# Projections that load x by columns, with means and deviations made a chunk ahead and spread through DRAM

## The chip, the cores and the metric

The program runs on one core of one Trainium2 chip. The metric is the device time of one execution in microseconds; three runs of the kernel before gave 1718.45 to 1718.74, with a median of 1718.49.

## The reference

A gated cross-attention block with a feed-forward part behind it, on 4 sequences of 1024 tokens with 512 features. This case is about its first lines, the projections:

```python
def _layernorm(x, axis=-1, eps=1e-05):
    m = jnp.mean(x, axis=axis, keepdims=True)
    v = jnp.var(x, axis=axis, keepdims=True)
    return (x - m) / jnp.sqrt(v + eps)
...
Q = heads(layernorm(x), Wq, bq)     # [4096 tokens, 512]
K = heads(ctx, Wk, bk)
V = heads(ctx, Wv, bv)
scores = Q @ K^T / sqrt(32) + adj;  scores = where(mask == 0, -inf, scores)
out = softmax(scores) @ V
x = x + tanh(g_xattn) * (out @ Wo.T + bo)
x = x + tanh(g_ffn) * ffn(layernorm(x))   # three cycles of a small network
```

## The kernel before

`project_phase` is the first of the program's stages; `attention_phase` and the feed-forward stage follow. The projections go through the 4096 tokens in 8 chunks of 512. For each chunk TensorE makes twelve products of 128 x 512 outputs (`acc`, four PSUM banks in turn): four of K from the context, four of V, four of Q from the normalised x. A product sums over four tiles t of 128 features, and every float32 operand is split into a high and a low part (`_hi`, `_lo`), so that each product is 4 x 3 = 12 matmuls (`three_pass`, L164 to L166): 144 matmuls a chunk. The context comes already with its features on the partitions (`ctxT`); x comes by rows (tokens on the partitions).

So x is normalised by rows and then turned on TensorE:

- VectorE's `norm_stats` reads the x rows of a chunk (`x_raw`) with BN_STATS and BN_AGGR, which give a mean and a variance for each token in `mv` (L448, L452).
- GpSimd's `inverse_std` makes 1/sqrt(variance + eps) in `rstd` (L256, L258).
- VectorE's `norm_apply` makes `xn` (L460), and TensorE turns it with 16 transposes of 128 x 128 into the PSUM tile `x_t` (L363), between the K and the V products.
- ScalarE makes `xT_hi` from it (L425), VectorE `xT_lo` (L497), and the Q products read both.

ScalarE also rounds each product into `out_hi` (L416) and the next context into `c_hi` (L402); VectorE makes `out_lo` (L488), `c_lo` (L465) and the V output (L503). Each of these reads frees a PSUM bank by `acc_read`; product n waits for the read of product n - 4. SyncE's queue stores the outputs.

GpSimd's queue loads x rows, context, mask and adjacency, and between the loads GpSimd builds one tile of `am` (the mask turned into a large negative number and added to adj) with two operations (`mask_tile`, L267 and L270). Its program runs in order: for chunk c it waits for `xn` of the chunk before, loads `x_raw` and `c_raw`, makes the deviations, loads mask and adjacency and builds. At c = 4 it also loads what the first attention group needs (`first_group`, L276 to L279).

Nothing plans this order at run time: each engine has its own written program, and semaphores join them. Chunks 1 to 7 are loops on SyncE and TensorE, chunks 1 to 6 on ScalarE and VectorE. The line that holds the turn in place on VectorE is, in `chunk`,

```python
if more:
    norm_stats(c + 1)
    split_context(c + 1)
    norm_apply(c + 1)
low_parts(c, 8, 4, bias_q)
```

## Time and profile before

| | |
|---|---|
| median of 3 runs | 1718.49 us |
| the profiled execution | 1718.82 us, its span 1717.0 us |
| TensorE (PE) busy | 1693.4 us, 99% |
| VectorE (DVE) busy | 1454.5 us, 85% |
| ScalarE (ACT) busy | 1270.9 us, 74% |
| GpSimd (POOL) busy | 663.3 us, 39% |
| projections, from the first record to the first matmul of the attention | 0 to 289.28 us |

PE's matmuls overlap in the records, so that the time which one takes in a row of them is the distance between two starts, not its own duration. PEld is TensorE's loading of weights. A timeline row says when an instruction (or a merged run of x of them) started and how long it ran, and in brackets how long its engine had been idle and who released it.

### The profile page before, as it was taken

The numbers are of one execution on the slowest core, as the hardware profiler recorded it, in microseconds if no ns is written. First come the engines' busy times: TensorE is split into PE (matmuls) and PEld (weight loads), VectorE is DVE, ScalarE is ACT, GpSimd is POOL, SyncE is SP. The second block draws the span as 40 slices with busy tenths as digits, with TensorE's granted clock in tenths as the row PEclk, the third lists the DMA queues.
The fourth block names the chain that finished last, engine by engine and source line by source line (L and its number), as shares of the span: only waits on it lengthen the run. The fifth ranks groups of instructions, "written<-read, shape, count | busy, mean of one in ns | idle before, by whom it ended". The sixth has DMA issues, their size and how long they took to land. (4 is left out here: it accounts for less than half of the span.)

```text
span 1717.0 us, 34356 instructions
## 1 busy us (share of the span) xinstructions
PE 1693.4 (99%) x12456; PEld 1295.8 (75%) x12456; DVE 1454.5 (85%) x2580; ACT 1270.9 (74%) x2249; POOL 663.3 (39%) x598
## 2 busy tenths in 40 slices
PE   9999999999999999999999999999999999999997
PEld 7888888777777777777777777777786685775873
DVE  6554554999999999999999999999778978969968
ACT  4222223999999999999999999999765576466557
POOL 3442341432368642487532796454323010100100
PEclk9999999999999999999999999999999999999998
DMA  7778675866366675378563676665424313411301
GB/s 281 273 243 295 226 265 169 191 166 155 103 180 180 133 169 130 113 211 179 130 162 97 183 189 131 150 136 152 150 67 160 90 50 98 139 50 50 114 25 50
DMA packets 162105, 258.92 MB, mean 151 GB/s; under 512 B 25616, under 2 KB 78096, under 8 KB 161952
## 3 DMA queue, kind: packets, MB, share of 16 engines
q1 hardware_dynamic: 110416, 158.84, 29.1%
q0 software_dynamic: 50960, 97.01, 24.7%
q8 instruction: 93, 1.52, 0.4%
q10 hardware_dynamic: 576, 1.05, 0.2%
q14 instruction: 60, 0.49, 0.1%
HBM read 168.47 MB, written 84.18 MB: 147 GB/s over the span
## 5 line engine op out<-in xcount | busy, mean ns | idle before, releaser
L1024 DVE CUSTOM_DVE_ANT_0 a_neg<-a_sc_ps,am 128x1024 f32<-128x1024 f32 x512 | 621.7, 1214 | 1.4 <-PE a_sc_ps L856 1.3
L964 ACT ACTIVATE a_prob<-a_neg,a_row_min 128x1024 f32<-128x1024 f32 x512 | 585.7, 1144 | 13.9 <-DVE a_row_min L1024 7.8
L870 PEld LDWEIGHTS a_tr_ps<-ident,a_prob 128*128 128x128 f32 x4096 | 461.0, 140 | 89.1 <-issue 53.2
L870 PE MATMUL a_tr_ps<-ident,a_prob 128*128 128x128 f32 x4096 | 519.8, 274 | 0.9 <-ACT a_probT L942 0.9
L999 DVE COPY a_probT<-a_tr_ps 128x512 f32<-128x512 f32 x512 | 350.7, 685 | 36.9 <-PE a_tr_ps L870 35.4
L942 ACT ACTIVATE a_probT<-a_tr_ps 128x512 f32<-128x512 f32 x512 | 304.0, 594 | 35.1 <-PE a_tr_ps L870 16.0
L752 POOL DMA_DIRECT2D a_q_st<-q_parts x144 | 79.8, 560 | 161.2 <-PE a_sc_ps L856 125.3
L856 PE MATMUL a_sc_ps<-k_first,a_q_st 96*128 96x512 f32 x384 | 126.2, 426 | 0.0
L856 PE MATMUL a_sc_ps<-a_k_st,a_q_st 96*128 96x512 f32 x384 | 126.0, 426 | 0.0
L890 PE MATMUL a_o_ps<-a_probT,a_v 128*32 128x256 f32 x2048 | 123.6, 382 | 0.6 <-ACT a_o L953 0.6
L890 PE MATMUL a_o_ps<-a_probT,v_first 128*32 128x256 f32 x2048 | 123.8, 382 | 0.0
L890 PEld LDWEIGHTS a_o_ps<-a_probT,a_v 128*32 128x32 f32 x2048 | 60.5, 109 | 55.9 <-ACT a_probT L942 12.0
L890 PEld LDWEIGHTS a_o_ps<-a_probT,v_first 128*32 128x32 f32 x2048 | 60.0, 109 | 56.1 <-DVE a_probT L999 11.6
L757 POOL TENSOR_SCALAR a_m_raw<-a_m_raw 128x1024 f32<-128x1024 int32 x24 | 87.0, 3632 | 27.0 <-DMA a_m_raw<-mask 26.8
L964 ACT ACTIVATION_READ_ACCUMULATOR a_prob<-a_neg,a_row_min 128x1 f32 x512 | 97.1, 190 | 0.0
L132 POOL TENSOR_TENSOR st_o<-st_o,st_rinv 128x512 f32<-128x512 f32 x32 | 41.5, 1298 | 114.4 <-DMA st_rinv<-rinv_all 114.3
L1711 DVE TENSOR_TENSOR f_B<-f_B,f_acc 128x512 f32<-128x512 f32 x64 | 43.7, 683 | 33.5 <-PE f_acc L166 24.3
L488 DVE SCALAR_TENSOR_TENSOR p_out_lo<-p_acc,p_bias_k,p_out_hi 128x512 fp32r<-128x512 f32 x32 | 23.7, 750 | 55.2 <-ACT p_out_hi L416 55.2
L416 ACT ACTIVATE p_out_hi<-p_acc,p_bias_q 128x512 fp32r<-128x512 f32 x32 | 21.9, 689 | 62.9 <-PE p_acc L166 62.9
L402 ACT ACTIVATE p_c_hi<-p_c_raw 128x2048 fp32r<-128x2048 f32 x7 | 13.4, 1918 | 72.7 <-PE p_acc L166 58.6
L1493 ACT ACTIVATE f_xn<-x,f_shift,f_rstd 128x512 f32<-128x512 f32 x32 | 23.5, 805 | 57.8 <-POOL f_shift L1296 57.8
L416 ACT ACTIVATE p_out_hi<-p_acc,p_bias_k 128x512 fp32r<-128x512 f32 x32 | 21.7, 689 | 58.6 <-PE p_acc L166 52.7
(236 smaller groups left out, 3364.2 us busy)
## 6 DMA issues: line engine op xcount, KB each, us to landing
a_q_st<-q_parts POOLq DMA_DIRECT2D x144, 128.0 KB, 4.0
k_first<-k_parts POOLq DMA_DIRECT2D x24, 512.0 KB, 7.9
a_k_st<-k_parts POOLq DMA_DIRECT2D x24, 512.0 KB, 7.9
a_m_raw<-mask SPq DMA_DIRECT2D x24, 512.0 KB, 5.0
a_adj_raw<-adj SPq DMA_DIRECT2D x24, 512.0 KB, 5.9
k_parts<-p_out_hi SPq DMA_DIRECT2D x32, 256.0 KB, 6.0
k_parts<-p_out_lo SPq DMA_DIRECT2D x32, 256.0 KB, 6.3
v_all<-p_v_out SPq DMA_DIRECT2D x8, 1024.0 KB, 4.4
```

The source lines that it names most:

```text
L132: pool.tensor_tensor(w.o[:], w.o[:], w.rinv[:], ALU.mult).then_inc(w.step, 1)
L416: act.activation(out_hi[:, m, :], acc[:, (n0 + m) % 4, :], ACT.Identity, bias=bias[:, m:m + 1]).then_inc(hi_ready, 1)
L752: pool.dma_start(q_st[qb][quad * D:(quad + 1) * D], src).then_inc(q_loaded[qb], 16)
L757: pool.tensor_scalar(m_raw[:, t % 2, :].bitcast(F32), m_raw[:, t % 2, :], 0.0, -BIG, ALU.is_equal, ALU.mult).then_inc(big_ready, 1)
L856: last = pe.matmul(sc_ps[:, r % 2, half * 512:(half + 1) * 512], q_st[qb][0:STACK, h, qt * P:(qt + 1) * P], k_st[par][0:STACK, h, half * 5 ...
L870: last = pe.transpose(tr_ps[:, bank(u, half), j * P:(j + 1) * P], prob[:, r % NPROB, t * P:(t + 1) * P], ident[:])
L890: last = pe.matmul(o_ps[h * D:(h + 1) * D, 0:QB], v_sb[vpar][:, t, h * D:(h + 1) * D], probT[:, prev % 2, h, t, :], start=(t == 0), stop=( ...
L942: act.activation(probT[:, (r // UB) % 2, h, 0:4, qt * P:(qt + 1) * P], tr_ps[:, bank(u, 0), :].rearrange("p (t q) -> p t q", t=4), ACT.Cop ...
L964: act.activation(prob[:, r % NPROB, :], neg[:, r % 2, :], ACT.Exp, scale=-1.0, bias=row_min[:, r % 2:r % 2 + 1], accum_out=row_sum[:, r // ...
L999: dve.tensor_copy(probT[:, (r // UB) % 2, h, 4:8, qt * P:(qt + 1) * P], tr_ps[:, bank(u, 1), :].rearrange("p (t q) -> p t q", t=4)).then_i ...
L1024: dve.tensor_tensor_reduce(out=neg[:, r % 2, :], in0=sc_ps[:, r % 2, :], in1=am[:, 2 * qb + qt, :], scale=-1.0, scalar=3.4e38, op0=ALU.add ...
L1711: dve.tensor_tensor(target[j][:, m, :], target[j][:, m, :], acc[:, 2 + step // 2, :], op).then_inc(shared_read, 1)
```

## The change

Chunk 0 goes as before. From chunk 1 on x is loaded by columns: a second input, `xT`, holds x with the features on the partitions, 512 tokens a chunk, and `x_cols` (the same memory as `xn`) takes it. The x rows are still loaded, for the means and variances alone. TensorE's 16 transposes of chunks 1 to 7 go. In their place:

- GpSimd's `inverse_std` writes mean and inverse deviation of a chunk's tokens into columns 0 to 3 and 4 to 7 of `norm_cols` (128 x 32), with a third small operation for the mean.
- VectorE's `turn_norm` turns `norm_cols` in squares of 32 x 32 into `norm_turned`.
- GpSimd stores it in DRAM with four DMAs of 8 x 32 elements (`store_norm`), waits until they have landed, and loads the two rows of 512 back into all 128 partitions (`spread_norm`, to `norm_rows`, in the second half of the memory of `stage[:, 0]`).
- VectorE subtracts the mean row (`centre`) and multiplies by the deviation row (`scale`), one operation of 128 x 512 each for each of the four feature tiles.
- ScalarE and VectorE split `x_cols` instead of `x_t`.

`norm_stats(c + 1)` stands at the start of chunk c, `turn_norm(c + 1)` after the second K output. GpSimd's program issues its loads first and builds the mask tile behind them; the three parts of `first_group` are apart, behind the masks of chunks 3, 4 and 5. The loops over chunks are written out. The two gates' loads count on `b_loaded`.

```diff
-                held_wait(pool, mv_ready, c + 1, pool_passed)
+                wait(pool, mv_ready, c + 1)
                 pool.tensor_scalar(var_eps[:], mv[:, :, 1], EPS, 1.0, ALU.add, ALU.mult).then_inc(var_ready, 1)
-                pool.wait_ge(var_ready, c + 1)
-                pool.tensor_tensor(rstd[:], var_eps[:], minus_half[:], ALU.pow).then_inc(rstd_ready, 1)
+                pool.tensor_scalar(mean, mv[:, :, 0], 1.0, 0.0, ALU.mult, ALU.add).then_inc(var_ready, 1)
+                pool.wait_ge(var_ready, 2 * c + 2)
+                pool.tensor_tensor(rstd, var_eps[:], minus_half[:], ALU.pow).then_inc(rstd_ready, 1)
...
+            def load_rows(c):
+                pool.wait_ge(stats_ready, c)
                 pool.dma_start(x_raw[:], x[ds(c * CH, CH), :].rearrange("(t p) e -> p t e", p=P)).then_inc(x_loaded, 16)
...
+            def load_columns(c):
+                pool.wait_ge(xT_lo_ready, ET * c)
+                pool.dma_start(x_cols[:], xT[c].rearrange("(t p) s -> p t s", p=P)).then_inc(xT_loaded, 16)
+
+            def store_norm(c):
+
                 inverse_std(c)
-                mask_tile(c)
+                pool.wait_ge(turned, c)
+                target = stat_rows[c].rearrange("k (t g j) -> g (k t) j", g=P // SQUARE, j=SQUARE)
+                for g in range(P // SQUARE):
+                    pool.dma_start(target[g], norm_turned[g * SQUARE:g * SQUARE + 2 * TT, :]).then_inc(norm_stored, 16)
+
+            def spread_norm(c):
+                wait(pool, scaled, ET * (c - 1))
+                pool.wait_ge(norm_stored, 64 * c)
+                pool.dma_start(norm_rows, stat_rows[c].partition_broadcast(P)).then_inc(norm_rows_loaded, 16)
+
+            inverse_std(0)
+            pool.wait_ge(xn_ready, 1)
+            load_rows(1)
+            load_context(1)
+            pool.wait_ge(w_lo_ready, 2 * ET)
+            load_mask(0)
+            load_columns(1)
+            store_norm(1)
+            load_rows(2)
+            spread_norm(1)
+            build_mask(0)
+            for c in range(1, NCH):
+                if c < NCH - 1:
+                    load_context(c + 1)
+                load_mask(c)
+                if c < NCH - 1:
+                    store_norm(c + 1)
+                    if c < NCH - 2:
+                        load_rows(c + 2)
+                    spread_norm(c + 1)
+                    load_columns(c + 1)
+                build_mask(c)
+                if c == 3:
+                    first_keys()
+                elif c == 4:
+                    first_queries()
+                elif c == 5:
+                    first_values()
...
-                pe.wait_ge(xn_ready, c + 1)
-                for t in range(ET):
-                    for s in range(TT):
-                        last = pe.transpose(x_t[:, t, s * P:(s + 1) * P], xn[:, s, t * P:(t + 1) * P], ident[:])
-                    last.then_inc(xT_ready, 1)
                 if first:
+                    pe.wait_ge(xn_ready, 1)
+                    for t in range(ET):
+                        for s in range(TT):
+                            last = pe.transpose(x_t[:, t, s * P:(s + 1) * P], xn[:, s, t * P:(t + 1) * P], ident[:])
+                        last.then_inc(xT_ready, 1)
...
-            with pe.Fori(1, NCH) as c:
+            for c in range(1, NCH):
                 chunk(c, False)
...
+                        act.wait_ge(scaled, ET * (c - 1) + t + 1)
+                        source = x_cols
+                    act.activation(xT_hi[:, t, :], source[:, t, :], ACT.Copy).then_inc(xT_hi_ready, 1)
...
+            def centre(c, t):
+                if t == 0:
+                    dve.wait_ge(xT_loaded, 16 * c)
+                    dve.wait_ge(norm_rows_loaded, 16 * c)
+                dve.tensor_tensor(x_cols[:, t, :], x_cols[:, t, :], norm_rows[:, 0, :], ALU.subtract).then_inc(centred, 1)
+
+            def scale(c, t):
+                dve.wait_ge(centred, ET * (c - 1) + t + 1)
+                dve.tensor_tensor(x_cols[:, t, :], x_cols[:, t, :], norm_rows[:, 1, :], ALU.mult).then_inc(scaled, 1)
...
+            def turn_norm(c):
+                dve.wait_ge(rstd_ready, c + 1)
+                wait(dve, norm_stored, 64 * (c - 1))
+                dve.transpose(norm_turned[:], norm_cols[:]).then_inc(turned, 1)
...
+                    if normalised:
+                        centre(c, m)
+                        if m:
+                            scale(c, m - 1)
+                        if m == 1 and c < NCH - 1:
+                            turn_norm(c + 1)
 
             def chunk(c, more):
-                low_parts(c, 0, 0, bias_k)
...
+                if c and more:
+                    norm_stats(c + 1)
+                low_parts(c, 0, 0, bias_k, c > 1)
+                if c == 1:
+                    turn_norm(2)
+                    for t in range(ET):
+                        centre(1, t)
+                        if t:
+                            scale(1, t - 1)
+                if c:
+                    scale(c, ET - 1)
...
-                    dve.tensor_tensor(xT_lo[:, t, :], x_t[:, t, :], xT_hi[:, t, :].bitcast(F32), ALU.subtract).then_inc(xT_lo_ready, 1)
...
+                    dve.tensor_tensor(xT_lo[:, t, :], (x_cols if c else x_t)[:, t, :], xT_hi[:, t, :].bitcast(F32), ALU.subtract).then_inc(xT_lo_ready, 1)
...
+                if c == 0:
+                    norm_stats(1)
                 wait(dve, v_stored, 16 * c)
                 for m in range(4):
                     dve.wait_ge(acc_ready, NACC * c + 4 + m + 1)
                     dve.tensor_tensor(v_out[:, m, :], acc[:, m, :], bv_rows[:], ALU.add).then_inc(acc_read, 1)
+                    if c == 0 and m == 1:
+                        turn_norm(1)
                 if more:
-                    norm_stats(c + 1)
                     split_context(c + 1)
-                    norm_apply(c + 1)
                 low_parts(c, 8, 4, bias_q)
```

VectorE, the second half of chunk 0, before: the outputs of V, then statistics, context and normalisation of chunk 1, then the low parts of Q.

```order
L497 TENSOR_TENSOR p_xT_lo<-p_x_t,p_xT_hi 128x512 x4
L503 TENSOR_TENSOR p_v_out<-p_acc,p_bv_rows 128x512 x4
L448 BN_STATS p_stats<-p_x_raw 128x6 x4
L452 BN_AGGR p_mv<-p_stats 128x2 x4
L465 TENSOR_TENSOR p_c_lo<-p_c_raw,p_c_hi 128x2048
L460 TENSOR_SCALAR p_xn<-p_x_raw,p_mv,p_rstd 128x512 x4
L488 SCALAR_TENSOR_TENSOR p_out_lo<-p_acc,p_bias_q,p_out_hi 128x512 x4
```

The same place in the changed kernel (`p_norm_cols` holds mean and inverse deviation).

```order
L574 TENSOR_TENSOR p_xT_lo<-p_x_t,p_xT_hi 128x512 x4
L495 BN_STATS p_stats<-p_x_raw 128x6 x4
L499 BN_AGGR p_mv<-p_stats 128x2 x4
L582 TENSOR_TENSOR p_v_out<-p_acc,p_bv_rows 128x512 x2
L543 STREAM_TRANSPOSE p_norm_turned<-p_norm_cols 128x32
L582 TENSOR_TENSOR p_v_out<-p_acc,p_bv_rows 128x512 x2
L521 TENSOR_TENSOR p_c_lo<-p_c_raw,p_c_hi 128x2048
L549 SCALAR_TENSOR_TENSOR p_out_lo<-p_acc,p_bias_q,p_out_hi 128x512 x4
L495 BN_STATS p_stats<-p_x_raw 128x6 x4
L499 BN_AGGR p_mv<-p_stats 128x2 x4
```

The statistics of chunk 1 moved ahead of V's outputs, the normalisation of rows is gone, and the next statistics stand behind the Q parts. In chunk 2 of the changed kernel VectorE's program reads as follows, from its third K output on; `p_xn` is the memory of `x_cols` and `p_stage` that of `norm_rows`.

```order
L543 STREAM_TRANSPOSE p_norm_turned<-p_norm_cols 128x32
L549 SCALAR_TENSOR_TENSOR p_out_lo<-p_acc,p_bias_k,p_out_hi 128x512
L513 TENSOR_TENSOR p_xn<-p_xn,p_stage 128x512
L517 TENSOR_TENSOR p_xn<-p_xn,p_stage 128x512
L549 SCALAR_TENSOR_TENSOR p_out_lo<-p_acc,p_bias_k,p_out_hi 128x512
L513 TENSOR_TENSOR p_xn<-p_xn,p_stage 128x512
L517 TENSOR_TENSOR p_xn<-p_xn,p_stage 128x512 x2
L574 TENSOR_TENSOR p_xT_lo<-p_xn,p_xT_hi 128x512 x4
L582 TENSOR_TENSOR p_v_out<-p_acc,p_bv_rows 128x512 x4
L521 TENSOR_TENSOR p_c_lo<-p_c_raw,p_c_hi 128x2048
```

Here the low parts of K have the two steps of normalisation between them, and `xT_lo` reads two tiles in SBUF. GpSimd's program for one chunk, before:

```order
L286 DMA p_x_raw<-x 128x4x512
L288 DMA p_c_raw<-ctxT 128x4x512
L256 TENSOR_SCALAR p_var_eps<-p_mv 128x4
L258 TENSOR_TENSOR p_rstd<-p_var_eps,p_minus_half 128x4
L263 DMA p_stage<-mask 128x1024
L264 DMA p_stage<-adj 128x1024
L267 TENSOR_SCALAR p_stage<-p_stage 128x1024
L270 TENSOR_TENSOR am<-p_stage 128x1024
```

And in the changed kernel:

```order
L292 DMA p_c_raw<-ctxT 128x4x512
L264 DMA p_stage<-mask 128x1024
L265 DMA p_stage<-adj 128x1024
L256 TENSOR_SCALAR p_var_eps<-p_mv 128x4
L257 TENSOR_SCALAR p_norm_cols<-p_mv 128x4
L259 TENSOR_TENSOR p_norm_cols<-p_var_eps,p_minus_half 128x4
L304 DMA stat_rows<-p_norm_turned 8x32 x4
L288 DMA p_x_raw<-x 128x4x512
L309 DMA p_stage<-stat_rows 128x1024
L296 DMA p_xn<-xT 128x4x512
L269 TENSOR_SCALAR p_stage<-p_stage 128x1024
L271 TENSOR_TENSOR am<-p_stage 128x1024
```

The two building operations went from behind their own loads to the end of the chunk's list, behind the load of the columns, and six DMAs are new.

## Rows read from the trace of the kernel before

**Rows 1.** The page: busy time by engine, then TensorE's granted clock in 40 slices.

```profile
PE 1693.4 (99%) x12456; PEld 1295.8 (75%) x12456; DVE 1454.5 (85%) x2580; ACT 1270.9 (74%) x2249; POOL 663.3 (39%) x598
...
PEclk9999999999999999999999999999999999999998
```

**Rows 2.** Busy time in a stretch, chunks 1 to 7.

```profile
core 0: us, PE busy (x) PEld busy (x) DVE busy (x) ACT busy (x) POOL busy (x), PEclk, DMA share, GB/s
...
44.00:286.00 242.00, 241.09 (x1119) 200.79 (x1119) 120.47 (x194) 63.75 (x92) 79.69 (x57) 1.00 0.70 248
```

**Rows 3.** Timeline of TensorE: first K product of chunk 2, its turn, first V product.

```profile
79.49 0.39 PE L164 MATMUL p_acc<-p_c_hi,p_w_hi 128*128 128x512 f32 x1
...
90.37 1.91 PE L363 MATMUL p_x_t<-ident,p_xn 128*128 128x128 f32 x16
92.04 0.47 PE L164 MATMUL p_acc<-p_w_hi,p_c_hi 128*128 128x512 f32 x1
```

**Rows 4.** Timeline of ScalarE: the context's high part, in chunks 2 and 3.

```profile
68.87 1.92 ACT L402 ACTIVATE p_c_hi<-p_c_raw 128x2048 fp32r<-128x2048 f32 x1 [10.06 <-PE p_acc L166]
...
103.31 1.92 ACT L402 ACTIVATE p_c_hi<-p_c_raw 128x2048 fp32r<-128x2048 f32 x1 [10.09 <-PE p_acc L166]
```

**Rows 5.** Timeline of TensorE: chunk 0's first Q product, into chunks 1 and 4.

```profile
33.17 0.39 PE L164 MATMUL p_acc<-p_xT_hi,p_w_hi 128*128 128x512 f32 x1
...
43.83 0.39 PE L166 MATMUL p_acc<-p_xT_lo,p_w_hi 128*128 128x512 f32 x1
44.95 0.49 PE L164 MATMUL p_acc<-p_c_hi,p_w_hi 128*128 128x512 f32 x1 [0.74 <-DVE p_out_lo L488]
...
148.11 0.39 PE L166 MATMUL p_acc<-p_xT_lo,p_w_hi 128*128 128x512 f32 x1
148.66 0.49 PE L164 MATMUL p_acc<-p_c_hi,p_w_hi 128*128 128x512 f32 x1 [0.17 <-DVE p_out_lo L488]
```

**Rows 6.** Timeline of VectorE in chunk 0.

```profile
26.12 2.47 DVE L497 TENSOR_TENSOR p_xT_lo<-p_x_t,p_xT_hi 128x512 fp32r<-128x512 f32 x4
...
33.98 2.46 DVE L448 BATCH_NORM_STATS2 p_stats<-p_x_raw 128x6 f32<-128x512 f32 x4
...
36.77 4.25 DVE L465 TENSOR_TENSOR p_c_lo<-p_c_raw,p_c_hi 128x2048 fp32r<-128x2048 f32 x1
42.24 1.91 DVE L460 TENSOR_SCALAR p_xn<-p_x_raw,p_mv,p_rstd 128x512 f32<-128x512 f32 x4 [1.22 <-POOL p_rstd L258]
```

**Rows 7.** Timeline of GpSimd: a mask tile, a blocked and an unblocked deviation.

```profile
32.75 3.66 POOL L267 TENSOR_SCALAR p_stage<-p_stage 128x1024 f32<-128x1024 int32 x1 [10.00 <-DMA p_stage<-mask]
36.49 2.40 POOL L270 TENSOR_TENSOR am<-p_stage 128x1024 f32<-128x1024 f32 x1
...
72.49 2.13 POOL L256 TENSOR_SCALAR p_var_eps<-p_mv 128x4 f32<-128x4 f32 x1 [17.22 <-DVE p_mv L452]
...
142.09 0.20 POOL L256 TENSOR_SCALAR p_var_eps<-p_mv 128x4 f32<-128x4 f32 x1 [16.06 <-DVE p_mv L452]
142.37 1.04 POOL L258 TENSOR_TENSOR p_rstd<-p_var_eps,p_minus_half 128x4 f32<-128x4 f32 x1
```

**Rows 8.** Timeline of VectorE in chunk 2, and two starts in chunk 0.

```profile
6.10 0.69 DVE L476 TENSOR_TENSOR p_w_lo<-p_stage,p_w_hi 128x512 fp32r<-128x512 f32 x1
6.70 0.68 DVE L474 TENSOR_TENSOR p_c_lo<-p_c_raw,p_c_hi 128x512 fp32r<-128x512 f32 x1
...
72.31 2.26 DVE L465 TENSOR_TENSOR p_c_lo<-p_c_raw,p_c_hi 128x2048 fp32r<-128x2048 f32 x1
...
91.30 0.75 DVE L488 SCALAR_TENSOR_TENSOR p_out_lo<-p_acc,p_bias_k,p_out_hi 128x512 fp32r<-128x512 f32 x1 [1.98 <-ACT p_out_hi L416]
```

**Rows 9.** The x rows' DMA issued at 19.19 us: KB, us from issue to landing.

```profile
p_x_raw<-x POOLq DMA_DIRECT2D x1, 1024.0 KB, 6.7
```

**Rows 10.** The context tile's DMA landings over all chunks; GpSimd's time for three issues.

```profile
DMA to landing us min/median/max: 4.1/10.1/16.3
...
L278 POOL DMA_DIRECT2D q_first<-q_parts x3 | 1.6, 552 | 0.0
```

110 lines of the change are left out of this document (54 added, 56 removed).

## The prediction

> **What bounds the kernel now.** I read the page first [rows 1]: TensorE is busy for 99% of the span at its upper clock (2.4 GHz, a granted clock of 0.9 or more in all slices but the last), and the other engines have room. The change is inside the projections, so I looked at that stretch alone [rows 2]: from 44 to 286 us TensorE is busy for 241.1 of 242.0 us, VectorE for 120.5, ScalarE for 63.8, GpSimd for 79.7, and the DMA engines are 0.70 busy at 248 GB/s. So here the end is set by what TensorE has to do, and only what is taken out of its queue, or put into it as a wait, moves the time. Behind the projections nothing is edited; TensorE stays the busy engine there, and its work starts when the projections end. An us saved ahead of it is an us saved.
>
> **What TensorE loses.** In chunk 2 the first K matmul starts at 79.49 and the 16 transposes start at 90.37, 48 matmuls later: 10.88 / 48 = 0.2267 us each [rows 3]. The first V matmul starts at 92.04, so the transposes hold the queue for 1.67 us. The whole cadence is better read from one event of each chunk: the context's high part starts at 68.87 in one and at 103.31 in the next [rows 4], 34.44 us. 144 matmuls are 144 x 0.2267 = 32.64 us. The rest, 1.80 us, is what a turn costs (the two or three matmuls behind it start a little apart: 0.13 us more than the 1.67). Seven chunks lose it: 7 x 1.80 = 12.6 us. The upper bound is this; the lower is 7 x 1.67 = 11.7.
>
> **Two stalls that go.** Into chunk 1 TensorE waits: the matmul ahead starts at 43.83, the next at 44.95, where 44.06 would be the cadence [rows 5]. What it waits for is the first low part of Q, which VectorE does at about 44.07 only, because the normalisation of rows stands ahead of it from 42.24, and before that the context's low part took 4.25 us [rows 6]. `norm_apply` goes out of this place, so the low part is made as soon as ScalarE's half is there. That is 0.89 us, and 0.1 for the slower start after it. Into chunk 4 it is 148.11 to 148.66 [rows 5]: 0.32 and 0.1. That one comes from the loads of the first group, put all at once ahead of x and context; they are now spread over three chunks. Together 1.4 us.
>
> **What is added, and what hides it.** On VectorE a chunk loses `norm_apply` (about 1.9 us [rows 6]) and gets eight operations of 128 x 512 with two inputs in SBUF. The same shape stood in chunk 0: starts at 6.10 and 6.70, so 0.6 us each [rows 8], 4.9 us for eight. 120.5 us in seven chunks becomes about 120.5 + 6 x 3 + 5, 144 of 228 us: there is room, so only the places matter. I count from the first K matmul of a chunk (t = 0), with times of chunk 2 [rows 3, 8]: K's last low part runs from 91.30 - 79.49 = 11.8 to 12.6; V's products are due from 13.6 on (no turn between now), Q's first matmul at 2 x 10.88 = 21.8, the next chunk at 32.6.
>
> Chunks 2 to 7: the last low part of Q ends 1.7 into the next chunk, as K's does after its product (92.05 against 90.37). The statistics take 36.77 - 33.98 = 2.8 us [rows 6], to 4.5. K's low parts then have centre and scale between them, 0.75 + 0.6 + 0.6 = 2.0 us for each 2.72 us of TensorE. After the last, scale ends at 14.4, ScalarE's last `xT_hi` at 15.0, `xT_lo` at 15.7: 6.1 us ahead of the Q products at 21.8. V's outputs then run from 15.7, their first bank needed at 21.8. The turn of the statistics waits for GpSimd: unblocked 0.2 + 0.2 + 1.04 = 1.4 us after 4.5 [rows 7], blocked twice as at 72.49 (2.13) it would be 5.3. VectorE comes to the turn at 8.3, so it waits between nothing and 1.5 us; the slack of 6.1 takes both. Nothing on the path.
>
> The turn itself has no row. It is not cheaper than nothing and the nearest whole operation, on a 16 times wider tile, is 0.6 us; I take 0.1, near the aggregation's size, and both bounds are inside the slack. The Trainium skill, "VectorE: DVE Perf Modes", section "The three transpose paths", gives 311 ns for a VectorE transpose of 128 x 128 in bf16, and no run here shows one yet; by that figure nothing in the sum changes either.
>
> Chunk 1 is tighter: all eight operations stand behind the K parts. 12.6 + 0.1 to 0.6 + 4.9, then 0.6 on ScalarE and 0.7 on VectorE for the last tile, gives 18.9 to 19.4, and with the first V output, 0.7 more, 19.6 to 20.1 against 21.8. Slack 1.7 us or more. I cost it at nothing.
>
> Chunk 0: the statistics of chunk 1 now stand ahead of V's outputs. `xT_lo` ends at 28.6 [rows 6]; the x rows land at 19.19 + 6.7 = 25.9 [rows 9], so the statistics end at 31.4 and the first V output at 32.1. Its bank is needed by the first Q matmul at 33.17 [rows 5]: slack 1.0. After the second V output VectorE waits for GpSimd's 1.4 us and turns, at about 33.2; the third output's bank is needed two products later, at 38.6. Nothing again, but this is the smallest slack for an event that rests on a DMA.
>
> GpSimd gets, a chunk, one small operation (0.2 us unblocked, 2.1 blocked), four small DMAs, a broadcast and a column load: six issues of 0.53 us as for q_first [rows 10], 3.2 us. 79.7 us in 242 leave room for 5. In order on its queue: the stores go out by 11, it waits for them to land before the broadcast, then loads the columns once `xT_lo` is done (15.7), then builds the mask, 3.65 + 2.40 us [rows 7], to about 23.5. The waits on landing hold only the column load and the mask behind them. Both loads are needed by VectorE's first centre of the next chunk, at 32.6 + 5.3 = 37.9: 21 us after issue, against landings of 4.1 to 16.3 us for a tile of that size [rows 10]. The data a chunk moves rises from 34.44 x 0.248 = 8.5 MB by 1.0 (columns) and 0.5 (broadcast) to 10.1 MB, in 32.6 us 310 GB/s; at the same GB/s a share that is a DMA share of 0.87. High, not full.
>
> **The shared port.** The mask's second operation ran from 36.49 to 38.89, and VectorE's `c_lo` beside it took 4.25 us in place of 2.26 [rows 6 to 8]; the other way round GpSimd's tiny operation took 2.13 us beside a `c_lo` in place of 0.20. So an operation with two SBUF inputs on VectorE and one on GpSimd do not run together. The change makes twelve more such operations on VectorE a chunk (centre, scale, and `xT_lo`, which read PSUM). That is why the mask's place counts: at 17.4 to 23.5 it lies beside V's outputs, which read PSUM and did not stretch, and ends before `c_lo` at 23.9 (the context's high part starts at 103.31 - 79.49 - 1.80 = 22.0 and takes 1.92 [rows 3, 4]). The Trainium skill says so too ("GPSIMD Engine Reference", section "Key points"): the two engines share SBUF interfaces, and VectorE's instructions with two SBUF inputs contend. The trace agrees, with 4.25 against 2.26 us; what it would do here is the second rival.
>
> **The sum.** 12.6 + 1.4 = 14.0 us out of 1717.0, added 0: a span of 1703.0. The profiled run took 1718.82, 0.33 above the median of the three; from the median, 1718.49 - 14.0 = 1704.5 us. Own range 1703.3 (both stalls larger than read) to 1706.
>
> **Rivals.**
> - *Early stalls*, chance 0.13. The slacks of 1.0 us in chunk 0 and 1.7 in chunk 1 are used up. For it: the x rows must land by 28.6, and a queue at 0.8 busy can be late; every us over the slack is an us of TensorE. Against: nothing new is queued ahead of that load. It gives 1 to 4 us back: 1705.5 to 1708.5.
> - *The port lock in every chunk*, 0.05. If the stores land late, GpSimd starts the mask at 23.9, as `c_lo` does. 23.9 + 6.05 + 2.26 = 32.2, then Q's first low part 0.75: 33.0 against 32.6. With VectorE's late parts following, 0.4 to 1 us in each of 6 chunks: 1707 to 1710.
> - *The round trip through DRAM is late*, 0.04, of which 0.02 slower than before. Place: VectorE's first centre of a chunk, behind which stand K's low parts that free TensorE's banks. Until 21 us after issue nothing waits; another 6 are hidden. The gain is gone when each of six chunks waits 14.0 / 6 = 2.3 us, a landing of 29.6 us; slower by 0.2% (3.4 us) from 30.1. The longest landing above was 16.3, with the first group's loads around it. It would give 1718 to 1725.
>
> 0.78 is left for the forecast. The range reaches to 1708.5, which takes in the early stalls. 0.2%, 3.4 us, is about what a measurement of this kernel can tell from no change. Faster by more 0.96, within it 0.02, slower 0.02.
>
> **What the changed profile would show.** The high part of the context every 32.64 us; no row of x_t after chunk 0; TensorE's first K matmul of chunk 1 at 44.06, not 44.95; the last Q matmul about 14 us earlier than now; the stretch behind it as long as before. A turn of 0.1 to 0.6 us; GpSimd's mask beside V's outputs. I am wrong if TensorE waits for `xT_lo` or a V output in chunks 0 or 1, if `c_lo` takes over 4 us in most chunks, or if the attention behind gets longer by what the projections lose.

## The result, and the profile after

The changed kernel takes 1706.75 us (median of 4 runs, 1705.89 to 1706.81) where the kernel before takes 1718.47 us on the same chip (4 runs, 1718.17 to 1718.74). The ratio is 0.9931, with a 95% interval of 0.9913 to 0.9948: faster, by 11.7 us. The forecast was 1704.5 us, 2.2 us too low, inside its range. The profiled execution took 1706.81 us, its span is 1705.0 us where 1717.0 stood, so the two profiles differ by 12.0 us, and 14.0 was forecast. Where the missing 2.0 us are is the main question here.

The page of the changed kernel answers to [rows 1]:

```profile
PE 1680.3 (99%) x12344; PEld 1283.1 (75%) x12344; DVE 1475.7 (87%) x2615; ACT 1272.9 (75%) x2249; POOL 680.1 (40%) x649
```

The reader is to see 112 matmuls fewer, 16 in each of seven chunks, and VectorE busier by 21 us while the whole is shorter. The busy time by stretch answers to [rows 2]; the first row is chunks 1 to 7, the second all that lies behind:

```profile
core 0: us, PE busy (x) PEld busy (x) DVE busy (x) ACT busy (x) POOL busy (x), PEclk, DMA share, GB/s
44.00:273.00 229.00, 229.00 (x1013) 189.63 (x1012) 142.50 (x228) 66.52 (x92) 99.47 (x102) 1.00 0.87 303
273.00:1705.00 1432.00, 1412.15 (x11153) 1060.67 (x11151) 1303.91 (x2339) 1188.47 (x2134) 565.85 (x520) 1.00 0.51 130
```

In 229 us TensorE never waits. VectorE went from 120.5 to 142.5 us (144 was forecast), GpSimd from 79.7 to 99.5, and the DMA engines to 0.87 (0.87 was forecast). Over chunks 1 to 3 alone, 44 to 142 us, their share is 0.94.

TensorE's timeline has the marks of the accounting. They are the first V product of chunk 0, the last matmul of chunk 0's Q and the first of chunk 1's K, the first Q product of chunk 1, the matmuls on the identity that follow the projections, and the first product of the attention:

```profile
22.50 0.47 PE L157 MATMUL p_acc<-p_w_hi,p_c_hi 128*128 128x512 f32 x1 [1.26 <-DVE p_out_lo L549]
...
44.16 0.39 PE L159 MATMUL p_acc<-p_xT_lo,p_w_hi 128*128 128x512 f32 x1
44.38 0.39 PE L157 MATMUL p_acc<-p_c_hi,p_w_hi 128*128 128x512 f32 x1
...
66.14 0.39 PE L157 MATMUL p_acc<-p_xT_hi,p_w_hi 128*128 128x512 f32 x1
...
272.86 2.17 PE L423 MATMUL p_x_t<-ident 128*128 128x128 f32 x18
275.90 1.15 PE L935 MATMUL a_sc_ps<-k_first,q_first 96*128 96x512 f32 x4 [0.87 <-PEq L167]
```

The gap into chunk 1 is gone: 0.22 us where 1.12 stood [rows 5]. Seven chunks take 272.86 - 44.38 = 228.48 us, 32.64 each, which is what 144 matmuls take by [rows 3]. The same marks in the kernel before:

```profile
22.17 0.47 PE L164 MATMUL p_acc<-p_w_hi,p_c_hi 128*128 128x512 f32 x1 [1.26 <-DVE p_out_lo L488]
...
286.48 2.17 PE L380 MATMUL p_x_t<-ident 128*128 128x128 f32 x18
289.28 1.16 PE L856 MATMUL a_sc_ps<-k_first,q_first 96*128 96x512 f32 x4 [0.63 <-PEq L174]
```

Four differences give the account:

| stretch | before | after | saved |
|---|---|---|---|
| start to chunk 0's first V product | 22.17 | 22.50 | -0.33 |
| from there to the end of the projections | 264.31 | 250.36 | 13.95 |
| from there to the attention's first product | 2.80 | 3.04 | -0.24 |
| from there to the end of the span | 1427.74 | 1429.11 | -1.37 |
| sum | 1717.02 | 1705.01 | 12.01 |

The stretch that the forecast costed gave 13.95 for its 14.0, and in these two profiles all that is missing lies in the three rows that it costed at nothing. These are two single executions: the kernel before took 263.36 us for the second row in another profile (**r2** below) and not 264.31, while the changed kernel took 250.37 again.

What was added, on VectorE in chunks 0 and 1: the V outputs that now follow the statistics, then a turn and the eight operations on the columns, the low parts, and the V outputs behind them.

```profile
31.63 1.26 DVE L582 TENSOR_TENSOR p_v_out<-p_acc,p_bv_rows 128x512 f32<-128x512 f32 x2
...
56.98 0.20 DVE L543 STREAM_TRANSPOSE p_norm_turned<-p_norm_cols 128x32 f32<-128x32 f32 x1
57.10 1.25 DVE L513 TENSOR_TENSOR p_xn<-p_xn,p_stage 128x512 f32<-128x512 f32 x2
...
61.89 2.49 DVE L574 TENSOR_TENSOR p_xT_lo<-p_xn,p_xT_hi 128x512 fp32r<-128x512 f32 x4
64.30 1.88 DVE L582 TENSOR_TENSOR p_v_out<-p_acc,p_bv_rows 128x512 f32<-128x512 f32 x3
```

A turn takes 0.20 us. Chunk 0's first V output ends at 32.3 and its bank is wanted by the first Q product at 22.50 + 11.0 = 33.5: 1.2 us to spare (1.0 was forecast). In chunk 1 the first V output ends at 64.98, and its bank is wanted at 66.14: 1.2 us to spare (1.7 was forecast). All this stayed hidden, by about one us. The forecast had the sum short in one place. It put a single `xT_lo`, 0.7 us, behind the last `scale`, but VectorE's program has all four there: 2.4 us, from 17.6 to 20.0 after the chunk's start. The same holds in chunks 2 to 7, where `xT_lo` ends at 16.9 and not at 15.7, and the first V output at 17.5: 4.3 us to spare, and 2.7 in chunk 4.

GpSimd's chain in chunk 0, the stores, the wait for their landing, the broadcast:

```profile
33.94 2.15 POOL L304 DMA_DIRECT2D stat_rows<-p_norm_turned  x4 [0.54 <-DVE p_norm_turned L543]
...
40.87 0.54 POOL L309 DMA_DIRECT2D p_stage<-stat_rows  x1 [3.98 <-DMA stat_rows<-p_norm_turned]
```

The DMA issues of the projections, three of them (KB each, median us from issue to landing):

```profile
p_xn<-xT POOLq DMA_DIRECT2D x7, 1024.0 KB, 7.9
...
p_stage<-stat_rows POOLq DMA_DIRECT2D x7, 512.0 KB, 5.1
...
stat_rows<-p_norm_turned POOLq DMA_DIRECT2D x28, 1.0 KB, 3.2
```

From the first store to the broadcast's issue it is 6.9 us, of which 4.0 are waiting, and some 5 more until it has landed, against 21 us of room.

### The profile page after: what moved, and what is told of

The parts are those of the page before. It is cut to its first block and busy times, and to the rows that moved or that the text cites. A ratio compares the mean times of both kernels' runs of the same rounds, so it can differ in the third digit from the quotient of the medians.

```text
span 1705.0 us, 33568 instructions
## 1 busy us (share of the span) xinstructions
PE 1680.3 (99%) x12344; PEld 1283.1 (75%) x12344; DVE 1475.7 (87%) x2615; ACT 1272.9 (75%) x2249; POOL 680.1 (40%) x649
## 5 line engine op out<-in xcount | busy, mean ns | idle before, releaser
L1790 DVE TENSOR_TENSOR f_B<-f_B,f_acc 128x512 f32<-128x512 f32 x64 | 43.7, 683 | 33.5 <-PE f_acc L159 24.3
L1572 ACT ACTIVATE f_xn<-x,f_shift,f_rstd 128x512 f32<-128x512 f32 x32 | 23.5, 806 | 58.4 <-POOL f_shift L1375 58.4
L935 PEld LDWEIGHTS a_sc_ps<-k_first,a_q_st 96*128 96x128 f32 x384 | 59.1, 190 | 8.0 <-issue 4.5
L935 PEld LDWEIGHTS a_sc_ps<-a_k_st,a_q_st 96*128 96x128 f32 x384 | 59.2, 190 | 6.7 <-issue 4.2
```

What stands on the lines that cost most here:

```text
L935: last = pe.matmul(sc_ps[:, r % 2, half * 512:(half + 1) * 512], q_st[qb][0:STACK, h, qt * P:(qt + 1) * P], k_st[par][0:STACK, h, half * 5 ...
```

## The experiments

The theory: 12.6 us are the turns and 1.4 the two stalls; nothing of the additions reaches TensorE; about 2 us are given back outside the costed stretch. The rivals: the gain comes from elsewhere (the order of loads, the written-out loops), or the additions cost something that a larger gain covers.

### The turns alone

**k1_idle_turns.** Into the changed kernel, 16 transposes of the identity where the turns stood. Nobody waits for them.

```diff
@@ chunk(c, first), TensorE @@
                     pe.wait_ge(w_lo_ready, 2 * ET)
+                else:
+                    for t in range(ET):
+                        for s in range(TT):
+                            pe.transpose(x_t[:, t, s * P:(s + 1) * P], ident[:], ident[:])
```

> The changed kernel with 16 transposes of the identity put back into TensorE's queue in chunks 1 to 7, between the K and the V products; they write x_t, which nobody reads there, and wait for nothing. My theory (the turns' 1.80 us in TensorE's queue is the gain): the context's high part comes every 34.44 us again, the first matmul of the attention 7 x 1.80 = 12.6 us later than in the changed kernel (275.90 to 288.5), the time 1706.75 + 12.6 = 1719.3 us. Rival (the gain is from the waits on VectorE, and the turns ran beside something): under 3 us more, about 1708. The part behind the projections (1429.1 us from the attention's first matmul to the end in the changed kernel, 1427.7 before) tells a second thing: it stays at 1429.1 if the written-out code or its place is what lengthens it, and goes to 1427.7 if it is the moment at which the projections end.

Measured: 1719.58 us (10 runs, 1719.06 to 1719.91), ratio 0.9999 [0.9990, 1.0009] to the kernel before, span 1718.1. Chunk 1 begins at 45.12 us here and the projections end at 286.08: 240.96 us where the changed kernel takes 228.48, so 12.48 for seven turns, 1.78 each (1.80 was forecast). A turn in its timeline, which is [rows 3] again:

```profile
56.01 1.91 PE L413 MATMUL p_x_t<-ident 128*128 128x128 f32 x16
57.68 0.48 PE L157 MATMUL p_acc<-p_w_hi,p_c_hi 128*128 128x512 f32 x1
57.99 0.40 PE L158 MATMUL p_acc<-p_w_hi,p_c_lo 128*128 128x512 f32 x1
```

The turn holds the queue for 1.67 us, as before. The matmuls behind it start 0.31 and 0.24 us apart where 0.227 is the cadence; that is the 0.1 us above the turn itself. With the turns put back nothing measurable of the whole gain is left. What the stalls had cost (0.5 to 1.5 us, see **k3** and **r2**) is eaten by what is given back behind the projections (1428.99 us here, so the length of that stretch does not hang on the moment at which the projections end), and by chunk 0, whose statistics were ready 0.58 us later in this execution than in the changed kernel's (aggregation at 15.69 against 15.11).

**k2_old_no_turns.** The other way round: the kernel before, without the transposes of chunks 1 to 7. Its Q in those chunks is made from what chunk 0 left in `x_t`; all other work is there.

```diff
@@ chunk(c, first), TensorE @@
-                for t in range(ET):
-                    for s in range(TT):
-                        last = pe.transpose(x_t[:, t, s * P:(s + 1) * P], xn[:, s, t * P:(t + 1) * P], ident[:])
-                    last.then_inc(xT_ready, 1)
+                if first:
+                    for t in range(ET):
+                        for s in range(TT):
+                            last = pe.transpose(x_t[:, t, s * P:(s + 1) * P], xn[:, s, t * P:(t + 1) * P], ident[:])
+                        last.then_inc(xT_ready, 1)
+                else:
+                    pe.sem_inc(xT_ready, ET)
```

> The kernel before with the transposes of chunks 1 to 7 taken out and nothing else: x_t keeps chunk 0's values, so Q of the other chunks is computed from chunk 0's x. xn is still made and waited for. My theory: 12.6 us less in the projections, with the 0.89 us stall into chunk 1 still there: the attention's first matmul at 289.28 - 12.6 = 276.7, the time 1718.47 - 12.6 = 1705.9 us, or up to 1 us more if other stalls appear. Rival (the column load and the new order on VectorE bring part of it): over 1709 us. Behind the projections: 1427.7 us if the loops keep it as before, 1429.1 if the earlier end of the projections is what costs.

Measured: 1708.31 us (4 runs, 1707.78 to 1712.58), ratio 0.9942 [0.9927, 0.9957], span 1706.5. The attention starts at 278.15 us, 11.1 earlier than in the kernel before; 12.6 was expected. The missing part is one stall, which grew from 0.32 us [rows 5] to 2.01; the one into chunk 1 is 0.45 in this execution, and was 0.89:

```profile
142.42 0.39 PE L166 MATMUL p_acc<-p_xT_lo,p_w_hi 128*128 128x512 f32 x1
144.66 0.49 PE L164 MATMUL p_acc<-p_c_hi,p_w_hi 128*128 128x512 f32 x1 [1.86 <-DVE p_out_lo L491]
```

VectorE tells why. The context of the next chunk lands late behind the loads of the first group (ScalarE has waited 14.01 us for it when it starts the high part at 137.74), so its high part, its low part and the normalisation of rows stand where Q's outputs should be (the first low part of Q starts at 143.79 only):

```profile
141.96 1.91 DVE L463 TENSOR_SCALAR p_xn<-p_x_raw,p_mv,p_rstd 128x512 f32<-128x512 f32 x4
```

A DMA does not get faster when TensorE does. Beside the turns the two stalls were worth up to 1.4 us; without the turns they are 0.45 + 2.01 = 2.5. `norm_apply`, 1.9 us, stands ahead of the low part in both. So a term for the stalls can be added only together with the 12.6 taken after it: the turns alone give 11.1, and the rest of the change gives what is missing. Whether `norm_apply` alone, or the spreading of the first group's loads alone, would have been enough without the turns was not run.

**k3_old_apply_later.** The kernel before, with the normalisation of rows moved behind Q's low parts.

```diff
@@ VectorE, chunk(c, more) @@
                     split_context(c + 1)
-                    norm_apply(c + 1)
                 low_parts(c, 8, 4, bias_q)
+                if more:
+                    norm_apply(c + 1)
```

> The kernel before with norm_apply of the next chunk placed behind the low parts of Q on VectorE. My theory: TensorE's stall into chunk 1 (0.89 us and 0.1 of slow start) goes, so its first K matmul there starts at about 44.06 + the shift of chunk 0 in this run, and the time is 1717.5 us, 1.0 less. Rival (what TensorE waited for is the context's low part, which took 4.25 us beside GpSimd's mask): the stall stays at 0.9 us and the time at 1718.5.

Measured: 1718.04 us (11 runs, 1717.54 to 1718.41), ratio 0.9990 [0.9981, 0.9999], span 1716.2. The attention starts 1.39 us earlier (1.4 was the term). Into chunk 1 no gap is left, though the context's low part is about as long as before beside GpSimd's mask (4.08 us at 36.86):

```profile
43.91 0.39 PE L166 MATMUL p_acc<-p_xT_lo,p_w_hi 128*128 128x512 f32 x1
44.14 0.39 PE L164 MATMUL p_acc<-p_c_hi,p_w_hi 128*128 128x512 f32 x1
```

Into chunk 4 none is left either, though the x rows landed as late as in the first profile (statistics at 138.94 us against 138.99). So both stalls need `norm_apply` in its old place. Stalls first and turns second, 1.39 + 12.48 = 13.9 us, is the 13.95 of the account.

But both need something else too, and that differs from execution to execution. The second profile of the kernel before (**r2**) has only 0.40 us of the first stall. TensorE, then `c_lo` on VectorE:

```profile
43.80 0.39 PE L166 MATMUL p_acc<-p_xT_lo,p_w_hi 128*128 128x512 f32 x1
44.43 0.49 PE L164 MATMUL p_acc<-p_c_hi,p_w_hi 128*128 128x512 f32 x1 [0.24 <-DVE p_out_lo L488]
```

```profile
36.75 3.76 DVE L465 TENSOR_TENSOR p_c_lo<-p_c_raw,p_c_hi 128x2048 fp32r<-128x2048 f32 x1
```

`c_lo` is 0.49 us shorter than in [rows 6], and so is the stall (0.40 for 0.89). So the rival of this run was half right: the stretching of `c_lo` beside the mask pushes `norm_apply` back, and with it the low part. The second stall is not there at all in **r2**: the x rows landed earlier (statistics at 137.74 us). Against this profile **k3** gains 0.42 us at the attention's start and not 1.39. In **k7** the two stalls are 0.31 and 1.04.

### The additions: how much room is left

**k6_norm_twice** (one execution). Each of VectorE's eight operations on the columns is made twice, the first time into `x_t`, which nobody reads.

```diff
@@ centre(c, t) and scale(c, t), VectorE @@
+                dve.tensor_tensor(x_t[:, t, :], x_cols[:, t, :], norm_rows[:, 0, :], ALU.subtract)
                 dve.tensor_tensor(x_cols[:, t, :], x_cols[:, t, :], norm_rows[:, 0, :], ALU.subtract).then_inc(centred, 1)
...
+                dve.tensor_tensor(x_t[:, t, :], x_cols[:, t, :], norm_rows[:, 1, :], ALU.mult)
                 dve.tensor_tensor(x_cols[:, t, :], x_cols[:, t, :], norm_rows[:, 1, :], ALU.mult).then_inc(scaled, 1)
```

> The changed kernel with centre and scale each made twice, the first time into x_t, which nobody reads after chunk 0: eight more operations of 0.6 us for VectorE in chunks 1 to 7. The doubles read the shared memory as the others do. My theory (slack of 1.7 us in chunk 1, 6.1 in the others): TensorE waits 4.9 - 1.7 = 3.2 us in chunk 1, up to 3.7, where xT_lo ended 1.8 us ahead of the Q products in the changed kernel; nothing in chunks 2 to 7. The projections end 3.2 to 3.7 us later. Rival (VectorE has no room in any chunk): 4.9 us in each of seven, 34 us.

Measured: 1712.68 us, span 1710.9; the attention starts at 282.39, 6.5 us later than in the changed kernel. Chunk 1, timeline of TensorE:

```profile
66.12 0.39 PE L159 MATMUL p_acc<-p_w_lo,p_c_hi 128*128 128x512 f32 x1
70.15 0.47 PE L157 MATMUL p_acc<-p_xT_hi,p_w_hi 128*128 128x512 f32 x1 [3.64 <-DVE p_v_out L584]
...
71.15 0.63 PE L157 MATMUL p_acc<-p_xT_hi,p_w_hi 128*128 128x512 f32 x1
71.58 0.63 PE L158 MATMUL p_acc<-p_xT_hi,p_w_lo 128*128 128x512 f32 x1
```

Eight more operations of 0.6 us move the first V output by 5.0 us (69.32 against 64.30); TensorE waits 3.80 us beyond its cadence, so 1.2 us had been to spare, as read above. Behind the wait it does not go on as before: the matmuls start 0.427 us apart in place of 0.227. The stretch by windows shows the granted clock, 0.58 of full speed over 4 us (0.5, which is 1.2 GHz, for 3.41 of them, and 2.4 GHz again after):

```profile
70.00:74.00 4.00, 3.85 (x10) 3.09 (x11) 3.99 (x5) 0.00 (x0) 3.92 (x2) 0.58 0.75 210
```

That costs 1.7 us on top, seven intervals of 0.20 and shorter ones at both ends. In chunks 2 to 6 there is no wait at all, but 4.9 us more work leave only 0.9 to 1.7 us to spare, and 0.2 in chunk 4. They move the first V output by 2.5 to 3.3 us only, since VectorE otherwise waits between K's low parts. There are 0.58 us of waiting in chunk 7, where one of the doubled operations took 2.89 us in place of 0.68 beside GpSimd's mask. Chunk 1 is the tight one, as forecast.

**k5_late_columns** (one execution). The column load of chunks 2 and later is held until the last product of the chunk before.

```diff
@@ load_columns(c), GpSimd @@
                 pool.wait_ge(xT_lo_ready, ET * c)
+                if c > 1:
+                    pool.wait_ge(acc_ready, NACC * c)
```

> The changed kernel with the column load of chunks 2 to 7 held until TensorE has finished the chunk before (GpSimd waits for its last Q product), about 16 us later than in the changed kernel; the mask behind it on GpSimd is late by the same. My theory (21 us until VectorE waits, 6 more until TensorE does): issued at 33 of the chunk before, with a landing of 7.9 us (the median of these loads in the changed kernel), so at 41, 8 us into the chunk, VectorE's first centre is 3 us late, xT_lo 3 us late, inside the 6: TensorE waits for nothing, the attention's first matmul at 275.9 as in the changed kernel. A landing of 11 us or more would show on TensorE, us for us. Rival (the round trip and the columns have no slack): the 8 us in each of six chunks show, the projections end 20 to 48 us later.

Measured: 1706.14 us, span 1704.3, no wait of TensorE from 30 to 275 us. In chunk 4 the columns are issued at 142.73 us, 0.7 after the chunk's first product and not 15.4 us ahead of it (126.85 in the changed kernel). GpSimd in that chunk, then VectorE:

```profile
142.73 0.76 POOL L298 DMA_DIRECT2D p_xn<-xT  x1 [11.55 <-PE p_acc L159]
...
171.93 0.55 POOL L311 DMA_DIRECT2D p_stage<-stat_rows  x1 [12.68 <-DMA stat_rows<-p_norm_turned]
```

```profile
152.02 0.69 DVE L515 TENSOR_TENSOR p_xn<-p_xn,p_stage 128x512 f32<-128x512 f32 x1 [4.80 <-DMA p_xn<-xT]
...
162.62 2.48 DVE L584 TENSOR_TENSOR p_v_out<-p_acc,p_bv_rows 128x512 f32<-128x512 f32 x4
```

VectorE waits 3.8 to 5.1 us in each chunk, its V outputs start at 162.62 where Q's first product is due at 163.75, and TensorE notices nothing. The room is there: 16 of the 21 us ahead of the first centre are taken away, the load lands 4.8 us too late for the centre, and what lies behind absorbs that. But it is less than the forecast's 6 us behind the centre: the first V output ends at 163.31, so 0.44 us are left, 5.2 in all. The four stores of 1 KB, issued from 156.29 us, once took over 12 us to land, and that stayed hidden too.

**k8_mask_at_c_lo** (one execution). GpSimd's mask is held until VectorE's `c_lo` begins: the rival of the port lock, forced.

```diff
@@ GpSimd, ahead of the mask @@
+                    pool.wait_ge(c_hi_ready, ET * (c + 2))
                 build_mask(c)
```

> The changed kernel with GpSimd's mask of chunks 1 to 6 held until the context's high part is made, the moment at which VectorE starts c_lo: the two meet at the shared port in each chunk. By the second rival's sum: if GpSimd goes first, c_lo ends at 32.2 and Q's first low part at 33.0 against the next chunk's 32.6, so TensorE waits 0.4 to 1 us in each of six chunks, 2 to 6 us in all; c_lo in place of 2.3 takes 6 to 8 us. If VectorE goes first, the mask's first operation takes 2 us more, c_lo its 2.3, and TensorE waits for nothing. I expect them to start together and one of the two to happen in nearly all chunks.

Measured: 1705.96 us, span 1704.2, no wait of TensorE. GpSimd, then VectorE:

```profile
133.31 3.65 POOL L269 TENSOR_SCALAR p_stage<-p_stage 128x1024 f32<-128x1024 int32 x1 [6.11 <-ACT p_c_hi L446]
```

```profile
133.32 3.18 DVE L522 TENSOR_TENSOR p_c_lo<-p_c_raw,p_c_hi 128x2048 fp32r<-128x2048 f32 x1 [1.41 <-ACT p_c_hi L446]
```

The mask's first operation, started with `c_lo`, stretches it by 0.9 us only (3.18 against 2.29, in all six chunks) and is not stretched itself. Neither the rival's full lock nor no effect at all. It is the mask's second operation, with two inputs, that shuts `c_lo` out; in this placement it comes at 137.05, when `c_lo` is over.

### Chunk 0

**k4_no_first_mean.** GpSimd leaves out the copy of the mean in chunk 0, whose mean goes nowhere.

```diff
@@ inverse_std(c), GpSimd @@
-                pool.tensor_scalar(mean, mv[:, :, 0], 1.0, 0.0, ALU.mult, ALU.add).then_inc(var_ready, 1)
-                pool.wait_ge(var_ready, 2 * c + 2)
+                if c:
+                    pool.tensor_scalar(mean, mv[:, :, 0], 1.0, 0.0, ALU.mult, ALU.add).then_inc(var_ready, 1)
+                pool.wait_ge(var_ready, 2 * c + 1)
```

> The changed kernel without GpSimd's third small operation (the mean's copy) in chunk 0, where nobody reads it. My theory: it stands on chunk 0's path (variance, deviation, xn, transposes, V), so xn of chunk 0 starts 0.28 us earlier (17.31 to 17.03), the projections end 0.3 us earlier, and the time is 1706.45 us, less than what a measurement tells. Rival: the start of V in chunk 0 hangs on the high part of Wv's low part on VectorE alone and nothing moves: first V matmul at 22.50 as in the changed kernel.

Measured: 1706.18 us (5 runs, 1706.09 to 1707.47), ratio 0.9925 [0.9911, 0.9938], span 1704.3. VectorE, first in the changed kernel, then here, from the aggregation of the variances to the rows of `xn`:

```profile
15.11 0.38 DVE L499 BATCH_NORM_AGGREGATE p_mv<-p_stats 128x2 f32<-128x6 f32 x4
17.31 1.92 DVE L506 TENSOR_SCALAR p_xn<-p_x_raw,p_mv,p_norm_cols 128x512 f32<-128x512 f32 x4 [1.82 <-POOL p_norm_cols L259]
```

```profile
14.65 0.38 DVE L500 BATCH_NORM_AGGREGATE p_mv<-p_stats 128x2 f32<-128x6 f32 x4
16.57 1.92 DVE L507 TENSOR_SCALAR p_xn<-p_x_raw,p_mv,p_norm_cols 128x512 f32<-128x512 f32 x4 [1.55 <-POOL p_norm_cols L260]
```

2.20 us in one, 1.92 in the other, and 1.93 in the kernel before: the copy is on the path, for 0.27 us.

**r3_no_first_mean** is the same kernel again, beside **r1_after_again**, the changed kernel, and **r2_before_again**, the kernel before, to see how much of this is one execution's luck.

> The changed kernel once more, for a second profile and for times beside the kernel before on this chip. The projections took 13.6 us less, but the stretch from the attention's first matmul to the end 1429.1 us in place of 1427.7, and I don't know why: over the ten profiles so far it was 1427.7 to 1429.1, in looped and written-out forms. Theory (it differs from execution to execution, not from kernel to kernel): the second profile gives another value in this span, and so does the kernel before. Rival (something in the changed program lengthens it): 1429.1 again, and 1427.7 again for the kernel before. Time 12 to 14 us under the kernel before.

> The kernel before once more, for a second profile. Execution theory: the stretch from the attention's first matmul to the end differs from the first profile's 1427.7 us, upward up to 1429.1. Rival, a property of the kernel: 1427.7 within 0.1. The attention's first matmul at 289.3 plus or minus 0.3.

> The changed kernel without the mean's copy in chunk 0, beside the changed kernel itself on one chip. My theory: 0.3 us less than it, about 1706.4 against 1706.7, too little for a verdict in the time, and in the profile 1.92 us from the end of the aggregation's start to xn, where the changed kernel has 2.20 (15.11 to 17.31). Rival: no difference in either.

Measured: the changed kernel 1707.8 us (5 runs, 1705.77 to 1707.9), ratio 0.9928 [0.9915, 0.9942]; without the copy 1706.06 (5 runs, 1706.01 to 1707.22), ratio 0.9923 [0.9909, 0.9936]; the kernel before 1719.05 (8 runs, 1718.1 to 1721.05), ratio 0.9999 [0.9988, 1.0009]. The changed kernel is 11.3 us under the kernel before here, where 12 to 14 were expected. Behind the projections the two executions of the changed kernel differ by 0.17 us and those of the kernel before by 0.50, so part of what the changed kernel loses there is one execution's luck; in this second pair 0.7 us are left. The step in the trace is there again, 2.20 against 1.93 us, but the intervals overlap almost wholly: 0.27 us is seen in a timeline, not in a time. The 1.7 us between the two medians are not explained by it and lie inside the scatter of the changed kernel's runs. In these profiles the start of chunk 0's aggregation alone moves between 14.65 and 15.86 us.

### The loops written out

**k7_old_written_out.** The kernel before, with the loops over chunks of TensorE, ScalarE, VectorE and SyncE written out.

```diff
@@ all four engines @@
-            with pe.Fori(1, NCH) as c:
+            for c in range(1, NCH):
@@ product(...), TensorE @@
-                        if isinstance(c, int):
-                            pe.wait_ge(w_lo_ready, t + 1)
```

The edit also takes a wait for Wk's low part out of TensorE's chunk 0, as the changed kernel does; with the loops gone, VectorE's counting on `dve_passed` falls away as well.

> The kernel before with its loops over chunks written out on SyncE, TensorE, ScalarE and VectorE, nothing else. What it tells: why the stretch behind the projections is 1429.1 us in the changed kernel and in two of its variants, but 1427.7 to 1428.4 in the kernel before and two of its variants. Theory formed on these runs (the written-out instructions, by their number or place, lengthen it): from the attention's first matmul to the end 1429.0, the matmul 272 rows on 35.4 us after the first and not 35.15. The projections as before, the time 1719.5. Rival (GpSimd's or VectorE's part of the change, such as what it leaves in flight): 1428 us as in the kernel before.

Measured: 1720.61 us (10 runs, 1720.05 to 1725.66), ratio 1.0014 [1.0004, 1.0024], span 1718.2. Slower by 1.2 us in the span (1.7 against **r2**) and by 2.4 in the ratio. Not all of it is behind the projections: the stall into chunk 4 is 1.04 us in this execution, because the x rows landed late (VectorE waited 1.56 us for them), and that is 0.7 to 1.0 us more than in the two profiles of the kernel before. The attention begins at 289.15 us. The wait for TensorE's sequencer ahead of it is the changed kernel's (0.86 against 0.87), not that of the kernel before (0.63), and the stretch behind takes 1429.05 us. The step that was expected 272 matmuls into the attention did not come, though: 35.18 us, where 35.4 was expected.

**k9_tensor_loop.** The changed kernel with TensorE's loop alone put back.

```diff
@@ TensorE @@
-            for c in range(1, NCH):
+            with pe.Fori(1, NCH) as c:
```

> The changed kernel with TensorE's chunks 1 to 7 as a loop again, the other engines written out. What it tells: whether the loop or its writing out is worth anything on TensorE. Theory: the projections as in the changed kernel (144 matmuls at 0.2267 us, 32.64 us a chunk, no gap where the loop goes back, as in the kernel before), the time within 0.5 us of it. Rival (the written-out instructions cost the 1.4 us behind the projections): from the attention's first matmul to the end 1427.7 us, the time 1.4 us less.

Measured: 1706.69 us (5 runs, 1706.06 to 1706.94), ratio 0.9924 [0.9911, 0.9938], span 1704.9. There is no gap where TensorE's loop goes back; the attention starts at 275.96 behind a wait of 0.86 for the sequencer, as with the loop written out, and 1428.98 us lie behind. So the 0.24 us are not made by TensorE's own loop. The two lengths, in all 14 profiles:

| kernels | sequencer wait ahead of the attention | attention's first product to the end |
|---|---|---|
| loops kept on the other engines (before, twice; k2, k3) | 0.63 | 1427.74, 1428.24, 1428.38, 1428.29; mean 1428.16 |
| before with loops written out (k7) | 0.86 | 1429.05 |
| after, twice, and its variants (k1, k4, r3, k5, k6, k8, k9) | 0.86 to 0.87 | 1428.47 to 1429.11; mean 1428.90 |

The timelines show what part of this is. Counted in matmuls from the attention's first, TensorE's starts drift from the kernel before by some hundredths of a us over hundreds of matmuls, except for a few single places where one start comes 0.1 to 0.4 us later and the delay stays. One such place, matmul 272 of the changed kernel, shows in the distance from twelve transposes to the product behind them. The kernel before, the changed kernel, **k6**:

```profile
323.21 1.48 PE L870 MATMUL a_tr_ps<-ident,a_prob 128*128 128x128 f32 x12
324.44 0.71 PE L856 MATMUL a_sc_ps<-k_first,a_q_st 96*128 96x512 f32 x2
```

```profile
309.85 1.47 PE L949 MATMUL a_tr_ps<-ident,a_prob 128*128 128x128 f32 x12
311.33 0.73 PE L935 MATMUL a_sc_ps<-k_first,a_q_st 96*128 96x512 f32 x2
```

```profile
316.34 1.47 PE L951 MATMUL a_tr_ps<-ident,a_prob 128*128 128x128 f32 x12
317.57 0.71 PE L937 MATMUL a_sc_ps<-k_first,a_q_st 96*128 96x512 f32 x2
```

1.23, 1.48 and 1.23 us. The places, with the size of each step against the kernel before:

| kernels | steps, at matmul (us) |
|---|---|
| loops kept on all engines: before again, k3 | none |
| loops kept on all engines: k2 | 2583 (0.18) |
| k7 | 993 (0.25), 2075 (0.25), 5885 and 5898 (0.11 and 0.12), 6965 (0.26) |
| after, twice, k1, k4, r3, k5, k8, k9 | 272 (0.26), 1354 (0.23), 10278 (0.34 to 0.38) |
| k6 | 5465 (0.27), 6547 (0.23) |

(Matmul 10278 lies in the feed-forward stage, the others in the attention.) The first pair lies 1082 matmuls apart in each of the three. The places stay where they are when TensorE's program is edited (k1, k9) or GpSimd's (k4, k5, k8), also when the attention begins 13 us later (k1), and they move when VectorE's gets 56 instructions more (k6). VectorE and ScalarE themselves show no step there.

## Why the prediction was right, and where it was off

- **7 x 1.80 for the turns: right.** Put back, they cost 12.48 us, 1.78 each. The reading that chose the whole cadence over the 1.67 us of the turn itself was the better one.
- **1.4 us of stalls: right for the execution that it was read from, too large by about half a us in the mean.** Against that profile it comes out (1.39 in k3; in the profile after 13.95 - 12.60 = 1.35), but reading and answer share the one profile of the kernel before. Its second profile has 0.40 us into chunk 1 and nothing into chunk 4, 0.95 us less in the stretch. That the term met its number is in part luck. The cause given for the second stall, the loads of the first group, was one of two: moving `norm_apply` alone also removes it (k3). Its size holds only beside the turns; without them it is 2.0 us (k2).
- **The additions at nothing in chunks 1 to 7: right.** No wait of TensorE; the slacks were 1.2 us in chunk 0 (forecast 1.0), 1.2 in chunk 1 (forecast 1.7), and 4.3 in chunks 2 to 7 but 2.7 in chunk 4 (forecast 6.1), counted to the end of the first V output, because four `xT_lo` stand behind the last `scale` and one was reckoned. Turn 0.20 us, inside its bounds, twice the value taken. The mask ended at 24.2 and `c_lo` began at 24.1 in chunks 2, 3, 5 and 6, where 23.5 and 23.9 were forecast: it cleared `c_lo` by nothing.
- **"An operation with two SBUF inputs on VectorE and one on GpSimd do not run together": too broad.** It holds for GpSimd's operation with two inputs, and for its small one when that comes second ([rows 7]). It does not hold for its operation with one input when that comes first (below). The changed kernel has a meeting with the mask's second operation in three of its chunks, 1, 4 and 7 (there a `centre` took 1.82 us in place of 0.68), all hidden. The rival of the port lock could not have happened as it was worked out: k8 forces its place and costs TensorE nothing.
- **Chunk 0's small operation: missed.** "Nothing again" looked at VectorE's and TensorE's slacks behind the first V product, and not at `inverse_std(0)`, which stands ahead of it on the path with one operation more. 0.27 us, shown by k4 and again by r3. "Chunk 0 goes as before", in the description of the change, has the same gap.
- **The step that failed: "Behind the projections nothing is edited", and so "An us saved ahead of it is an us saved".** The mechanism holds, its size was off by 1.6 us: 0.24 at the boundary and 1.37 behind it. The sum had no term for the written-out loops. The 0.24 goes with loops written out on engines other than TensorE: it is in all ten profiles that have them, k7 among them, and in none of the four without. It is not TensorE's own loop (k9). Of the 1.37, about 0.5 is one execution's luck (the kernel before again: 1428.24), and 0.87 is the three steps of 0.26, 0.23 and 0.38 us. Steps of this size are in every profile with loops written out, also in k7, which has next to nothing else of the change, at the same matmuls in every execution of a program; of the three that keep the loops and were compared, two have none and k2 one of 0.18. So they go with the written-out programs, as far as 13 profiles can show it. Why they fall where they do, and which fetch or which queue makes them, stays open: k6 shows only that their places move with the length of VectorE's program. No kernel with everything changed but all loops kept was run.

The forecast's own terms, as measured: 13.95 - 0.33 - 0.24 - 1.37 = 12.0 us in the two profiles; with the mean of two executions of the kernel before for the first term (263.84 - 250.37 = 13.47), k4's 0.27, and the means of the table for the last (1428.90 - 1428.16 = 0.74), 13.47 - 0.27 - 0.24 - 0.74 = 12.2. The medians gave 11.7 on one chip and 11.3 on another. What is left is within what the changed kernel scatters from run to run (1705.77 to 1707.9).
